# Second attention of a two-layer gated kernel: two PSUM banks for transposed probabilities, two for projections

## What is computed

```
x = x + tanh(g_xattn[0]) * attention0(layernorm(x), ctx, mask0)
x = x + tanh(g_ffn[0])   * experts0(layernorm(x))
x = x + tanh(g_xattn[1]) * attention1(layernorm(x), ctx, mask1)
x = x + tanh(g_ffn[1])   * experts1(layernorm(x))
```

```
Q = einsum('bqd,hdk->hbqk', q, w_qs); K = einsum('bsd,hdk->hbsk', k, w_ks)
V = einsum('bsd,hdv->hbsv', v, w_vs)
attn = softmax(where(mask, -inf, einsum('hbqk,hbsk->hbqs', Q, K) / 16))
lin = concat_heads(einsum('hbqs,hbsv->hbqv', attn, V)) @ W_o.T + b_o
z = lin + q; out = (z - mean(z)) / (std(z) + 0.001) * gamma + beta
```

## Time and profile before

| | us |
|---|---|
| median of 3 executions | 1751.7 (1749.01 to 1755.86) |
| the profiled execution, its own time | 1754.9 |
| its span, first to last instruction | 1753.2 |
| units ahead of the loop | 805.3 to 837.5 |
| second attention, iterations 0 to 7 | 837.5 to 1456 |

### The profile page before, as it was taken

One profiled execution on the slowest core, in us unless ns is written; L12 is line 12 of the kernel. 1 busy time (PEld: TensorE's weight loads), 2 busy tenths in 40 slices (PEclk: granted clock), 3 DMA queues, 4 the chain that ended last, 5 costly groups with the idle time before them and its releaser, 6 DMA issues. The chain is left out here.

```text
span 1753.2 us, 35389 instructions
## 1 busy us (share of the span) xinstructions
PE 1344.4 (77%) x10568; PEld 1050.3 (60%) x10569; DVE 972.9 (55%) x3206; ACT 816.6 (47%) x2219; POOL 310.4 (18%) x337
## 2 busy tenths in 40 slices
PE   3788888887506999815999999999999993229980
PEld 2555555565405888804777787777778773216650
DVE  3778888887313545444666666665666665302223
ACT  3566666676303544413655554555555554113320
POOL 2323232321061000071100000000100000240006
PEclk9889989998557999957999999999999996559995
DMA  5700000000022332022000000000000000721113
GB/s 147 317 22 18 25 25 25 25 13 2 1 60 100 143 121 108 22 76 78 20 11 11 11 9 10 10 10 10 12 17 0 1 1 1 289 64 63 63 58 106
DMA packets 42625, 92.24 MB, mean 53 GB/s; under 512 B 10204, under 2 KB 30876, under 8 KB 39260
## 3 DMA queue, kind: packets, MB, share of 16 engines
q1 hardware_dynamic: 32468, 77.37, 12.7%
q0 software_dynamic: 8192, 13.15, 2.6%
q10 hardware_dynamic: 1872, 0.68, 0.2%
HBM read 66.18 MB, written 24.97 MB: 52 GB/s over the span
## 5 line engine op out<-in xcount | busy, mean ns | idle before, releaser
L507 ACT ACTIVATE b_prob<-b_prob,b_low 100x361 f32<-100x361 f32 x256 | 155.0, 606 | 106.4 <-DVE b_low L596 106.4
L943 PE MATMUL a_ps_t<-ident,a_prob 100*128 100x100 f32 x768 | 125.7, 276 | 60.3 <-ACT a_prob_t L1039 55.8
L943 PEld LDWEIGHTS a_ps_t<-ident,a_prob 100*128 100x128 f32 x768 | 84.1, 151 | 126.0 <-issue 61.5
L364 PE MATMUL b_ps_p<-b_context_part,b_wk_part 128*128 128x362 f32 x768 | 157.8, 342 | 0.0
L1031 ACT ACTIVATE a_prob<-a_prob,a_low 100x361 f32<-100x361 f32 x256 | 150.7, 591 | 13.2 <-DVE a_low L1144 12.9
L1039 ACT COPY a_prob_t<-a_ps_t 128x300 f32<-128x300 f32 x256 | 102.9, 402 | 110.7 <-PE a_ps_t L943 110.6
L515 ACT COPY b_prob_t<-b_ps_t 128x300 f32<-128x300 f32 x256 | 103.5, 404 | 105.3 <-PE b_ps_t L420 102.6
L370 PE MATMUL b_ps_p<-b_wv_part,b_context_part 128*128 128x512 f32 (+1 forms) x576 | 151.5, 405 | 0.0
L596 DVE CUSTOM_DVE_ANT_0 b_prob<-b_ps_s,b_mask_bias 100x361 f32<-100x361 f32 x256 | 121.8, 531 | 47.0 <-PE b_ps_s L410 30.7
L1144 DVE CUSTOM_DVE_ANT_0 a_prob<-a_ps_s,a_mask_bias 100x361 f32<-100x361 f32 x256 | 121.4, 531 | 30.5 <-PE a_ps_s L933 22.9
L420 PE MATMUL b_ps_t<-ident,b_prob 100*128 100x100 f32 x768 | 117.1, 261 | 20.0 <-ACT b_prob_t L515 19.5
(11 more groups left out here) (202 smaller groups left out, 2619.6 us busy)
## 6 DMA issues: line engine op xcount, KB each, us to landing
rows_in<-zero SPq DMA_DIRECT2D x16, 512.0 KB, 14.3
w<-in_c_fc SPq DMA_DIRECT2D x8, 1024.0 KB, 6.6
w<-in_c_proj SPq DMA_DIRECT2D x8, 1024.0 KB, 4.9
f_w<-in_W SPq DMA_DIRECT2D x2, 4096.0 KB
a_context<-in_ctx SPq DMA_DIRECT2D x16, 361.0 KB, 3.4
b_context<-in_ctx SPq DMA_DIRECT2D x16, 361.0 KB
f_xe<-rows_in SPq DMA_DIRECT2D x8, 512.0 KB, 3.8
rows_out<-f_ye SPq DMA_DIRECT2D x8, 512.0 KB, 2.7
```

Of the source, the lines that this page charges most:

```text
L364: ins = nc.tensor.matmul(bank[:, 0:LN2], w_parts["k"][a][:, k, t * P:(t + 1) * P], cx_parts[s][b][:, k, :], start=m == 0, stop=m == DK * l ...
L507: nc.scalar.activation(prob[0:S, k, 0:L], prob[0:S, k, 0:L], ACT.Exp, bias=low[0:S, k:k + 1], scale=-1.0, accum_out=total[0:S, k:k + 1]).t ...
L943: ins = nc.tensor.transpose(ps_t[:, c * S:(c + 1) * S], prob[0:S, k % QUAD_PB, c * P:(c + 1) * P], T["ident"][0:S, 0:S])
```

## The change

Two edits, both in the second attention. The transposed probabilities get two banks, used by head parity: the wait ahead of a transpose of head k is for the copy of head k-2, and ACT reads the bank of the head's parity. The units get two banks in place of three (`SECOND_BANKS` = 2): a unit waits for the unit two before it. The number of banks in all stays 8. The "none" unit in step 0, which fills the 38 units of an iteration up to a multiple of three, goes, since 38 is even. The first attention is as it was.

```diff
--- before.py
+++ after.py
@@ -145,6 +145,7 @@
 STEPS = PAIR_STEPS // 2
 LAG_TURN, LAG_VALUE = 1, 2
 PAIR_PB, PAIR_PT = 8, 8
+SECOND_BANKS = 2
 
 
 def second_schedule(last):
@@ -170,7 +171,7 @@
         at[half + (1, 1, 2, 3, 3, 3)[m]].append(("V", 0, t, p))
     at[half + LAG_VALUE].append(("W", 0, 0, 0))
     at = at[:STEPS]
-    for k in range(-sum(len(slot) for slot in at) % BANKS):
+    for k in range(-sum(len(slot) for slot in at) % SECOND_BANKS):
         at[k].append(("none", 0, k, 0))
     return Units(layer, [u for slot in at for u in slot], at)
 
@@ -203,9 +204,9 @@
     pt = sb("prob_t", [P, PAIR_PT, KT_N * S])
     ot = [sb(f"out_t{s}", [P, H // 2, S]) for s in range(2)]
     ps_s = [ps(f"ps_s{k}") for k in range(4)]
-    ps_t = ps("ps_t")
+    ps_t = [ps(f"ps_t{k}") for k in range(2)]
     ps_o = [ps_s[2 + g][:, LN2:LN2 + S] for g in range(2)]
-    ps_p = [ps(f"ps_p{k}") for k in range(BANKS)]
+    ps_p = [ps(f"ps_p{k}") for k in range(SECOND_BANKS)]
 
     full, final = second_schedule(False), second_schedule(True)
     half = STEPS // 2
@@ -255,7 +256,7 @@
         return part == -1 and isinstance(i, int) and i == 0
 
     def bank_of(u, before):
-        return ps_p[(u - n_pre if before else u) % BANKS]
+        return ps_p[(u - n_pre if before else u) % SECOND_BANKS]
 
     def units_of(sched, p):
         return sched.slots[p]
@@ -335,7 +336,7 @@
                 before = sched is pre
                 bank = bank_of(u, before)
 
-                back = u - BANKS
+                back = u - SECOND_BANKS
                 if before:
                     if back >= 0:
                         eng, k = pre.owner[back]
@@ -415,9 +416,9 @@
                 k = 4 * v + m
                 pe.wait_ge(normed.sem, normed.at(j, k + 1))
 
-                pe.wait_ge(pt_ready.sem, pt_ready.at(j, k))
+                pe.wait_ge(pt_ready.sem, pt_ready.at(j, k - 1))
                 for c in range(KT_N):
-                    ins = nc.tensor.transpose(ps_t[:, c * S:(c + 1) * S], prob[0:S, k % PAIR_PB, c * P:(c + 1) * P],
+                    ins = nc.tensor.transpose(ps_t[k % 2][:, c * S:(c + 1) * S], prob[0:S, k % PAIR_PB, c * P:(c + 1) * P],
                                               T["ident"][0:S, 0:S])
                 ins.then_inc(turned.sem, 1)
 
@@ -512,7 +513,7 @@
                 act.wait_ge(turned.sem, turned.at(j, k + 1))
 
                 act.wait_ge(valued.sem, valued.at(j, k // 2 + 1 - PAIR_PT // 2))
-                nc.scalar.copy(pt[:, k % PAIR_PT, :], ps_t[:, 0:KT_N * S]).then_inc(pt_ready.sem, 1)
+                nc.scalar.copy(pt[:, k % PAIR_PT, :], ps_t[k % 2][:, 0:KT_N * S]).then_inc(pt_ready.sem, 1)
 
             def steps(i, sched):
                 for p in range(len(sched.slots)):
```

## The result

| | before | changed |
|---|---|---|
| median, us | 1750.4 (1748.8 to 1755.9, 4 executions) | 1792.6 (1788.7 to 1795.0, 4 executions) |
| ratio | | 1.0234, 95% interval 1.0203 to 1.0264 |
| the profiled execution, its own time | 1754.9 | 1788.7 |
| loop iteration, mean of six | 79.47 | 85.29 |
| iteration 0, start to start | 71.3 | 77.4 |

A forecast was written before the change was run, and what follows sets the result against it. PE bounds the second attention, so new PE waits lengthen it one for one: 44 us in seven full iterations, +0.5 and -4.5 in the final one, +4 ahead of the loop, +44 us in all, 1796 us; range 1778 to 1810.

The forecast's parts named there:

- Third unit of steps 5 to 7: PE waits before the step's third unit (u2) for the first unit's low part: 0.51 us each, 1.53 for three.
- the tail: Ends of steps 4 to 7: the V or K behind a Q waits for u2's low part, 4.30 us per iteration.
- steps 0 and 1: Step 0 loses its 1.35 us wait, but later chains take most back: -0.1 us for both steps together.
- What the second transpose bank brings: Transposes stop waiting for ACT's copy out of the single bank; 19.4 us is all this edit can win.
- final iteration: Second attention's final iteration: steps 1 to 3 cost +0.5 us, steps 5 to 10 gain 4.5 of 5.4 us of waits.
- Ahead of the loop: Units before the loop, with two banks: 1.8 us more for K, 2 for Q, 0.2 for V; 4 us taken.
- The sum: Whole kernel: 44 us for seven full iterations, +0.5 and -4.5 final iteration, +4 ahead of the loop; 44 us slower.
- Two banks are enough: Rival: evacuation ends within the next unit's matmuls, so only transpose waits go; -19.4 us, 1732; chance 0.04.
- no change: Rival: a balance within 0.5%, needing most of the tail waits hidden too; chance 0.02.
- Tail waits alone: Rival: freed transposes move ACT ahead, so u2's waits and the light steps' drop out; +29 us, 1781; chance 0.15.
- The clock falls: Rival: more, shorter PE gaps put one step per iteration at the lower clock; +84 us, 1880; chance 0.04.

The follow-up runs named there:

- The experiment on the tail: Changed kernel, with ACT making the third unit's high part before the copy of the step's last transpose, not after: 1762.5 us, ratio 1.0083.
- The last experiment: Kernel before, loop written out, odd heads from 17 on in the final iteration transposed into the third unit bank: 1730.9 us, ratio 0.9876.

## Why the prediction was right

**Third unit of steps 5 to 7 and the tail.** Right in place, releaser and size. By the tables of the two iterations (before, the one from 1146.74 to 1226.60; us):

| step | before | changed | difference | forecast |
|---|---|---|---|---|
| 0 and 1 | 16.38 | 15.92 | -0.46 | -0.1 |
| 2 | 9.41 | 9.69 | +0.28 | +0.2 |
| 3 | 9.02 | 9.39 | +0.37 | +0.41 |
| 4 | 9.88 | 10.85 | +0.97 | +1.09 |
| 5 | 10.21 | 11.68 | +1.47 | +1.58 |
| 6 | 12.27 | 13.72 | +1.45 | +1.58 |
| 7 | 12.69 | 14.13 | +1.44 | +1.58 |

The sum for this pair of iterations is 5.5, for the mean of six 5.8; the forecast was 6.3. Two terms were mis-sized. A release took 0.06 us and not 0.10, at nine places 0.36. And steps 0 and 1 gave back 0.36 more than I took in this pair, 0.14 more in the mean of six, for a chain on DVE and ACT that I had bounded and not followed. The experiment on the tail gives the four tail waits 3.9 of the 4.3 us forecast.

**What the second transpose bank brings.** Right: in steps 0 and 7 the removed waits turned into waits for the outputs and for u2. Undoing that edit alone showed it, 8 to 12 us for waits of 19.4. In the final iteration PE waits 1.3 us for copies in the changed kernel (us, times), where 5.4 stood:

```profile
  ACT b_prob_t L516: 1.3, 3
```

The iteration is 4.7 us shorter, 4.0 forecast (-4.5 and +0.5). Some of that is the clock: with one bank it fell in these steps in the profile of before (0.60 from 1429 to 1431) and in that of the kernel with the first edit undone; with two it did not in any. Two pairs of profiles at full clock, both with the loop written out, part the waits from the clock. The last experiment took this iteration from 65.44 to 61.44 us: 4.0 for the waits alone, where I had 4.5. The change as a whole took it from 65.44 to 62.25: 3.2 for a forecast of 4.0. So some 1.5 of the 4.7 us were the clock of one execution, which the forecast did not have.

**Ahead of the loop.** The eight K of the changed kernel, which answer to the earlier trace rows:

```profile
816.16 9.47 PE L365 MATMUL b_ps_p<-b_context_part,b_wk_part 128*128 128x362 f32 x48
```

9.47 us for 8.25, so 1.2 for the K units; I had said 1.8. From the first K to the first scores the six profiles with two unit banks have 18.8 to 18.9 us and the four with three 17.3: 1.6 for K and V, where I had 2.0. From the first Q to the first K the six have 12.3 us on average and three of the four 10.4 (9.0, 10.8, 11.5), so 1.9 where I had 2; the fourth is the profiled execution of before with 15.0. For the whole part this pair of profiles shows -0.5 where I had +4. The six profiles with two unit banks have 30.9 to 31.7 us from the first unit to the first scores, the three others with three banks 28.1, 28.8 and 26.2, so it costs 2 to 5 us and the forecast of 4 holds. It is the profiled execution of before that was slow, 32.3, for another reason (last section).

**The sum.** What the profiles show for the terms is 41.0 us for the seven full iterations (44 forecast), -4.7 for the final one (-4.0) and 3.5 ahead of the loop (4), in all 39.8 for 44. The medians differ by 42.3. The 2.5 us between are placed nowhere by the profiles; executions of one kernel in the table above lie up to 7 us apart. The forecast is nearer to the medians than its terms are to theirs, and that much is luck.

**Rivals.** "Two banks are enough" and "no change" fell with the measurement. "Tail waits alone" fell with the table: step 6 has both waits. "The clock falls": at 1.00 in every step, with twelve waits in an iteration. The Trainium skill, page "Perfetto Trace Analysis", section "Matmuls", asks that groups rotate through banks so that the evacuation of one overlaps the next group; the case agrees with its aim and shows how many banks it takes: with two, the evacuation of K ended 1.0 us after PE was through with the next group, as long as ACT made the high part behind T3. The Trainium skill, page "TensorE: Matmul & The Clock Gate", section "A second HAM failure mode: psum-queue depth-cycling", tells of swings of the clock when TensorE idles briefly between groups that cycle through PSUM. In seven full iterations they did not show, at waits of at most 1.3 us. In the final iteration of kernels with one transpose bank the clock did fall in some profiles: in step 5 of the kernel before PE was busy for 5.32 of 6.78 us at a clock of 0.82. The same step with the loop written out had 4.25 of 5.70 us in one profile and stood at 1.00, so what decides is open.

## What to carry to other kernels

A bank is worth what its wait costs at the point where the consumer comes late, and that point is found by setting, for each unit, the end of its evacuation against the start of the unit n places on. A wait seen on the bound engine is not a gain if the engine next meets something else that was late for the same reason; ask what it meets. Before buying a bank, look at the order of the engine that empties it: here one exchange on ACT was worth 30 us. At the end of a stage banks can change their use.

## What was not expected of the hardware

A written-out loop gained 1.9 us per iteration in the mean of six, and 2.1 in the five that follow a jump. Of these 2.1 us 1.4 are in step 0 (DVE 0.93 us behind the scores for 2.21), and the rest is mostly in steps 3 and 7, behind the operations addressed by the counter. At what part of the jump or the address it arises was not tried.

DVE's split of a weight took 4.36 us for 2.36 beside POOL in the profile of the kernel before:

```profile
810.83 4.36 DVE L649 TENSOR_TENSOR b_wv_part<-b_values,b_wv_part 128x1024 fp32r<-128x1024 f32 x2
```

on POOL at that time, 1.59 us long when alone:

```profile
811.77 2.34 POOL L307 TENSOR_TENSOR b_context_part<-b_context,b_context_part 128x722 fp32r<-128x722 f32 x1 [0.18 <-POOL b_context_part L304]
```

and in the profile of the changed kernel, where the two do not meet:

```profile
806.38 2.36 DVE L650 TENSOR_TENSOR b_wv_part<-b_values,b_wv_part 128x1024 fp32r<-128x1024 f32 x2 [0.30 <-ACT b_wv_part L538]
...
809.56 1.59 POOL L308 TENSOR_TENSOR b_context_part<-b_context,b_context_part 128x722 fp32r<-128x722 f32 x1 [0.18 <-POOL b_context_part L305]
```

That is 2.00 us more on DVE and 0.75 on POOL. Where DVE's split had begun first it kept its 2.36 us, and POOL's cast of the context, 0.79 us long otherwise, took 1.44 (changed kernel, from 807.94) and 1.60 (before with the loop written out). It comes and goes between executions, with the arrival of the context and of the weights. It is not all that made this part slow in that execution. The first weight came late too:

```profile
807.27 1.99 ACT L537 CAST b_wk_part<-b_values 128x1024 fp32r<-128x1024 f32 x2 [8.97 <-DMA b_values<-in_wk]
```

This cast starts 1.98 us behind the first Q, and in the nine other profiles 0.4 to 0.7 us ahead of it. The 2.6 us of that and the 2.0 of the split make the 4.6 us by which this part was longer (32.3) than in the mean of the three others with three banks (27.7). The Trainium skill, page "SBUF — State Buffer", section "Who interferes with whom", says that DVE and GpSimd share one pair of ports, held by one of them at a time; that both engines were slowed where they met agrees with it, but no run was made to show that this is the cause.
